# Four graph layers in one launch on one core: the order of norms, biases and kept rows in layer 1, and which banks the sums of layers 3 and 4 use

## The chip, the core and the metric

The kernel runs on 1 core of a Trainium2 chip. The metric is the device time of one launch in microseconds (us). Before the change it is 790.58 us, the median of 3 runs (789.51 to 792.78).

## What is computed

x is 2048 x 256 (f32) and adj is a 2048 x 2048 matrix of zeros and ones. Four layers follow one another, each with a residual and a layer norm:

```python
x = _layernorm(x + _L0_gnn_ref(x, adj, weight, bias, node_w, edge_w))
x = _layernorm(x + _L1_gnn_ref(x, adj, adj, W_sa, a_sa, W_gcnb, b_gcnb, Wa, ba, Wb, bb))
x = _layernorm(x + _L2_gnn_ref(x, adj, weight2))
x = _layernorm(x + _L3_gnn_ref(x, adj, W1, b1, W2, b2, W3, b3))
# layer 1: h = x @ edge_w; e = where(adj > 0, h @ h.T, NEG_BIG)
#   out = (adj * softmax(x @ node_w, axis=0) * softmax(e, axis=1)) @ (x @ weight) + bias
# layer 2: attention over edges plus a plain graph convolution, both gated
# layer 3: relu((D^-1/2 (adj + I) D^-1/2) @ (x @ W))
# layer 4: h = relu(adj @ (x @ W1) + b1); h = relu(adj @ (h @ W2) + b2); adj @ (h @ W3) + b3
```

The code counts layers from 0: `weighted`, `final0` and `round0` are of layer 1, and `aggregate(1, ...)` and `aggregate(2, ...)` of layers 3 and 4.

## The kernel before

Rows of x are cut in 16 tiles of 128 (T = 16) and in 4 blocks of 512 (B = 4, TB = 4 tiles to a block). All order is written out by hand: one instruction stream to each engine, with semaphores between them. PSUM has 8 banks.

**Layer 1** goes tile by tile, t = 0 to 15. TensorE (PE) computes `scores(t)` (line 665), one row tile of h h^T, into banks 0 to 3. The matrix is symmetric, so ScalarE (ACT) keeps the part right of the diagonal in `keep_row(t)` (line 999), and later rows turn it instead of computing it. `make_fill(t)` (line 991) makes the mask from a row tile of adj that GpSimd (POOL) loads in `load_adj` (line 502). VectorE (DVE) adds the mask and takes the maximum in `maxima(t)` (line 1355). ACT takes the exponential (`exp_row`, line 1015) and its f16 high part (`p_high`, line 1020), and DVE the low part (`p_low`, line 1332). SP turns both with DMA transposes (`turn_p`, line 429). `weighted(m)` (line 687) multiplies them with the projected x into bank 6 or 7. `final0(m)` (line 1339) reads that bank, adds x and the bias (`xb`, which POOL makes in `bias_x`, line 497), and takes the moments. POOL makes the reciprocal deviation in `norm_factor` (line 489), and DVE applies it in `normed` (line 1287). PE's turn t is `scores(t)`, then `weighted(SUMMED[t])`, where SUMMED[t] is t - 3 from t = 4 on and 0 for t = 2; `scores(t)` waits for the maximum of t - 1 (`e_read`), and `weighted(m)` for `final0(m - 2)` (`pv_read`). DVE's round t (`round0`, line 1404) is maxima(t), p_low(t - 1), final0 of the tile summed in PE's turn t - 1, then its norm.

Before round 2 stands the start: transposes and projections (`group0`, line 640) through banks 4 to 7, then an exchange of maxima over the partitions on POOL, of which the scale of `sup` is made (lines 1427 to 1435).

**Layers 3 and 4** aggregate block by block. `aggregate(layer, b, f)` (line 783) sums over all 16 tiles, for feature half f = 0 or 1, in bank 4 + f. ACT and DVE take it apart in a high and a low part (`agg_high`, line 1097; `agg_low`, line 1481), and PE goes on with `out2(b)` (line 859) in layer 3 and with `hidden1(b)` and `rows(b)` (lines 880, 891) in layer 4. A sum may start when `agg_lo` says that its bank has been read. Blocks 1 to 3 are a loop on each engine (`Fori`), with this order on PE:

```python
with pe.Fori(1, B) as b:
    aggregate(2, b, 0)
    hidden1(b - 1)
    rows(b - 1, W2s, HID)
    aggregate(2, b, 1)
```

## Time and profile before

| | before |
|---|---|
| median of 3 runs | 790.58 us (789.51 to 792.78) |
| the profiled execution, its own time | 791.85 us |
| its span, first to last instruction | 790.0 us |
| mean granted TensorE clock | 0.988 |
| PE busy | 744.8 us (94%) |
| DVE busy | 452.6 us (57%) |
| ACT busy | 347.4 us (44%) |
| POOL busy | 120.0 us (15%) |

Times in rows count from the start of the span. PE is TensorE's matmuls, DVE VectorE, ACT ScalarE, POOL GpSimd, SPq the DMA queue of SyncE. A bracket at the end of a row of the timeline gives the idle time of the engine before the instruction, and what ended it. Granted clock 1.00 is 2.4 GHz, 0.50 is 1.2 GHz. Layer 1 lasts until 213 us, layer 2 until 391, layer 3 until 463, layer 4 until the end.

### The profile page before, as it was taken

How to read it: one execution, taken by the hardware profiler on the slowest of the kernel's cores; microseconds unless marked ns; L12 is line 12 of the kernel's file. 1: busy time of each engine (PE TensorE's matmuls, PEld its weight loads, DVE VectorE, ACT ScalarE, POOL GpSimd, SP SyncE). 2: the span in 40 equal slices, each digit the busy share in tenths (PEclk: the TensorE clock that was granted, in tenths of full speed). 3: DMA queues.
4: the chain of work that ended last, by engine and by line, in shares of the span. 5: the costliest groups of instructions: out<-in, count | busy, mean ns of one | idle time of the engine just before them, and what ended most of it. 6: DMA issues, size and time to landing. Idle time of an engine off the chain costs nothing.

```text
span 790.0 us, 11567 instructions
## 1 busy us (share of the span) xinstructions
PE 744.8 (94%) x4192; PEld 489.8 (62%) x4192; DVE 452.6 (57%) x934; ACT 347.4 (44%) x530; POOL 120.0 (15%) x246
## 2 busy tenths in 40 slices
PE   7888999797999999999989999999999999999997
PEld 6776766564678878787835545675664546465343
DVE  4485888688768797988944475121271311114465
ACT  4678877675385474646722243132270322224000
POOL 2011222111321012111122340000001000000343
PEclk9998999998999999999999999999999999999999
DMA  8948889996568509400030000000000000000011
GB/s 230 180 91 146 162 164 159 167 155 112 103 95 153 88 2 159 68 2 1 1 87 1 0 0 1 1 0 0 0 0 27 1 1 0 0 0 0 21 41 46
DMA packets 114300, 48.71 MB, mean 62 GB/s; under 512 B 103504, under 2 KB 109776, under 8 KB 114256
## 3 DMA queue, kind: packets, MB, share of 16 engines
q1 hardware_dynamic: 110224, 33.44, 21.7%
q0 software_dynamic: 4032, 14.68, 11.2%
q8 instruction: 27, 0.44, 0.2%
q14 instruction: 17, 0.14, 0.1%
HBM read 35.53 MB, written 2.10 MB: 48 GB/s over the span
## 4 chain that ended last, share of the span: by engine, by line
PE 43%; DVE 7%; issue 3%; ACT 1%; POOL 1%; DVEq 0%; POOLq 0%; ACTq 0%
PE ps L777 11%; PE ps L928 11%; PE ps L904 8%; PE ps L963 4%; PE ps L937 3%; PE ps L887 3%; PE ps L953 2%; DVE stats L1297 1%; PE ps L633 1%; DVE es_lo L1285 1%; DVE x L1575 1%; DVE tm L1495 1%; DVE agg_lo L1483 1%; DVE y L1619 0%; DVE y L1697 0%
## 5 line engine op out<-in xcount | busy, mean ns | idle before, releaser
L777 PE MATMUL ps<-adjT,x 128*128 128x512 bf16 (+1 forms) x768 | 173.3, 379 | 5.1 <-DVE agg_lo L1483 2.5
L777 PEld LDWEIGHTS ps<-adjT,x 128*128 128x128 f16 x768 | 72.3, 98 | 90.4 <-issue 7.6
L696 PE MATMUL ps<-sup,turned 128*128 128x512 f16 x256 | 88.3, 393 | 12.1 <-DVE y L1350 12.1
L1285 DVE TENSOR_TENSOR hh_lo<-hf,hh_hi 128x512 fp32r<-128x512 f32 x32 | 22.2, 693 | 134.5 <-ACT hf L1221 133.5
L928 PE MATMUL ps<-adjT,G 128*128 x384 | 83.6, 379 | 0.4 <-ACT hf L1221 0.4
L819 PE MATMUL ps<-H_hi,es_hi 128*128 128x258 f32 x256 | 76.8, 300 | 2.2 <-DVE es_lo L1285 1.7
L819 PE MATMUL ps<-H_lo,es_hi 128*128 128x258 f32 x256 | 72.4, 283 | 0.0
L819 PE MATMUL ps<-H_hi,es_lo 128*128 128x258 f32 x256 | 72.4, 283 | 0.0
L698 PE MATMUL ps<-sup,turned 128*128 128x256 f16 x256 | 71.7, 280 | 0.0
L928 PEld LDWEIGHTS ps<-adjT,G 128*128 128x128 f16 x384 | 37.3, 98 | 45.4 <-issue 0.9
L492 POOL TENSOR_TENSOR rstd<-mv,epsc 128x1 f32<-128x1 f32 x64 | 15.2, 238 | 295.9 <-DVE mv L1299 295.9
L1106 ACT ACTIVATE es_hi<-tm 128x1024 fp32r<-128x1024 f32 x32 | 33.9, 1059 | 52.6 <-DVE tm L1495 52.4
L696 PEld LDWEIGHTS ps<-sup,turned 128*128 128x128 f16 x256 | 25.7, 100 | 46.9 <-DVE y L1350 14.8
L819 PEld LDWEIGHTS ps<-H_hi,es_hi 128*128 128x128 f32 x256 | 48.3, 189 | 7.7 <-DVE es_lo L1285 4.7
L819 PEld LDWEIGHTS ps<-H_lo,es_hi 128*128 128x128 f32 x256 | 48.5, 189 | 0.4
L819 PEld LDWEIGHTS ps<-H_hi,es_lo 128*128 128x128 f32 x256 | 48.3, 189 | 0.0
L1285 DVE TENSOR_TENSOR es_lo<-tm,es_hi 128x1024 fp32r<-128x1024 f32 x32 | 39.2, 1225 | 14.9 <-issue 6.8
L1483 DVE SCALAR_TENSOR_TENSOR agg_lo<-ps,agg_hi 128x512 fp32r<-128x512 f32 x24 | 16.0, 685 | 52.3 <-ACT agg_hi L1099 52.3
L1328 DVE CUSTOM_DVE_ANT_0 em<-ps,fill 128x1024 f32<-128x1024 f32 x32 | 38.0, 1217 | 13.9 <-ACT kept L1006 7.8
L1495 DVE SCALAR_TENSOR_TENSOR tm<-slrow,ex,nb 128x512 f32<-128x512 f32 x64 | 45.3, 749 | 1.1
L1219 ACT ACTIVATE hh_hi<-ps,b2c,g 128x512 fp32r<-128x512 f32 x16 | 12.5, 779 | 72.2 <-PE ps L928 48.1
L963 PE MATMUL ps<-x,adjT 128*128 128x512 f16 x192 | 41.8, 379 | 1.9 <-DVE y L1699 1.9
(216 smaller groups left out, 1484.7 us busy)
## 6 DMA issues: line engine op xcount, KB each, us to landing
adjb<-in_adj POOLq DMA_DIRECT2D x16, 512.0 KB, 7.0
adjf<-in_adj POOLq DMA_DIRECT2D x12, 512.0 KB, 6.4
x<-in_x SPq DMA_DIRECT2D x4, 512.0 KB, 6.0
out<-adjf SPq DMA_DIRECT2D x16, 128.0 KB, 1.7
adjf<-in_L_gnn_W SPq DMA_DIRECT2D x1, 1024.0 KB, 5.9
W1f<-in_L_gnn_W SPq DMA_DIRECT2D x1, 512.0 KB, 3.7
adjf<-in_L_gnn_W SPq DMA_DIRECT2D x1, 512.0 KB, 3.9
we<-in_L_gnn_edge_w SPq DMA_DIRECT2D x1, 256.0 KB, 3.8
```

Source lines behind the costliest of these rows:

```text
L696: ins = mm(bank(6 + u), PT(HI, t)[:, jt, :], sup[:, jt, :], start=(jt == 0), stop=False, skip_group_check=True)
L698: ins = mm(bank(6 + u, D), PT(LO, t)[:, jt, :], sup[:, jt, 0:D], start=False, stop=(jt == T - 1), skip_group_check=True)
L777: ins = mm(bank(4 + f), x16[:, part, jt, f * P:(f + 1) * P], adj(b, jt), start=(jt == 0 and part == HI), stop=(jt == T - 1 and part == LO))
L819: ins = mm(bank(k, D + 2), es[p][:, (b * T + jt) % RE, k * P:(k + 1) * P], H[q][:, jt, :], start=(jt == 0 and (p, q) == (HI, HI)), stop=(j ...
L904: ins = mm(bank(to, width), hh[p][:, o, k * P:(k + 1) * P], ws[q][:, o, :], start=(o == 0 and (p, q) == (HI, HI)), stop=(o == KH - 1 and p ...
L928: ins = mm(bank(4 + o), g16(jt, part, o * P, P), adj(b, jt), start=(jt == 0 and part == HI), stop=(jt == T - 1 and part == LO))
L963: ins = mm(bank(u), adjT[:, bass.ds(b, 1), jt, k * P:(k + 1) * P].rearrange("p a c -> p (a c)"), f16[:, jt, :], start=(jt == 0), stop=(jt ...
L1106: own.link(run(es[HI][:, s, :], tm[:, s, :], ACT.Exp, scale=SLOPE - 1.0))
L1285: return tt(to, frm, high.bitcast(F32), ALU.subtract)
L1328: nc.vector.tensor_tensor_reduce(out=em[:, u, cols], in0=banks, in1=fill[:, t % 2, cols], scale=1.0, scalar=-3.0e38, op0=ALU.add, op1=ALU.max,
L1483: stt(agg[LO][:, f, :], bank(4 + f), 1.0 / XS, agg[HI][:, f, :].bitcast(F32), ALU.mult, ALU.subtract).then_inc(agg_lo, 1)
L1495: stt(tm[:, (b * T + jt) % RE, :], slrow[:, b * CB:(b + 1) * CB], ex[:, jt, 0:1], nb[:, jt % 2, :], ALU.add, ALU.max).then_inc(tm_ready, 1)
```

## The change

In layer 1:

- x's first block is loaded in two transfers, and the first transposes wait for the first of them (`x_first`) alone.
- `scores(0)` waits block by block for the part of h that it reads, not for all of it.
- On ACT, the mask of tile 1 is made after all projections, row 1 is kept before the exponential of the node weights, row 2 before the exponential of row 1, and row 3 before that of row 2.
- On DVE, the maximum of row 1 stands before the node maximum and the scale. In each round the norm of the former tile stands behind the maximum, and `final0` is of the tile that PE sums in the same turn, at the round's end.
- On POOL the first two biases are added before the exchange, adjacency row 5 is loaded behind it, and row tile 4 for layer 2 is loaded in step 9, not 5. SP turns that tile after all turns of layer 1.

In layers 3 and 4 the sums of odd blocks use banks 6 and 7, those of even blocks 4 and 5; a sum waits for the reading of the block two before. The loops over blocks are written out, the diagonal's waits are per block, and in layer 4 the last of block 2's row tiles stands behind block 3's second sum.

```diff
@@ sums
+        def agg_bank(layer, b, f):
+            return 4 + f + (2 * (b % 2) if layer else 0)
...
-                        wait_from(pe, agg_lo, (layer * B + b) * KD + f - 1)
+                        n = layer * B + b
+                        if n == B + 1:
+                            pe.wait_ge(g_ev, B * TB)
+                        else:
+                            wait_from(pe, agg_lo, (n - 1 if n <= B else n - 2) * KD + f + 1)
...
-            pe.wait_ge(diag_gone, T)
             pe.wait_ge(wp_ready, 2)
-            with pe.Fori(1, B) as b:
+            for b in range(1, B):
+                pe.wait_ge(diag_gone, TB * (b + 1))
                 aggregate(2, b, 0)
                 hidden1(b - 1)
-                rows(b - 1, W2s, HID)
+                rows(b - 1, W2s, HID, tiles=range(TB - (b == B - 1)))
                 aggregate(2, b, 1)
+            rows(B - 2, W2s, HID, tiles=(TB - 1,))
@@ layer 1, VectorE
             def round0(t):
-                u = t % 2
-                maxima(t, u)
-                p_low(t - 1, 1 - u)
-                m = SUMMED.get(t - 1)
-                if m is not None:
-                    final0(m, m % 2)
-                conv_first(LOW_ROUND.get(t, ()))
-                if m is not None:
-                    normed(m, m % 2, x[:, m, :])
+                maxima(t, t % 2)
+                if t - 1 in SUMMED:
+                    m = SUMMED[t - 1]
+                    normed(m, m % 2, x[:, m, :])
+                p_low(t - 1, (t - 1) % 2)
+                conv_first(LOW_ROUND.get(t, ()))
+                if t in SUMMED:
+                    final0(SUMMED[t], SUMMED[t] % 2)
@@ layer 1, the rest
-    LATER_LOADED = {5: 4}
+    LATER_LOADED = {9: 4}
...
+                    if t == 0:
+                        pe.wait_ge(p0_lo, P0.index(("h", c, KD - 1)) + 1)
...
-                if t == T - 2:
-                    sp.wait_ge(e_mm, B * T)
-                    turn_later(TB)
+            sp.wait_ge(e_mm, B * T)
+            for t in (TB, TB + 1):
+                turn_later(t)
```

**DVE, round 8 of layer 1, before** (`em,mx` is the masked maximum, `pl` the low part, `y` and `stats` are of `final0`, `x<-y` is the norm):

```order
L1328 ISA em,mx<-ps,fill 128x1024 [waits s_kept,fill_ready,e_mm]
L1328 ISA mx 128x1
L1328 ISA em,mx<-ps,fill 128x1024 [waits e_mm,s_kept]
L1328 ISA mx 128x1
L1362 TENSOR_SCALAR negm<-mx 128x1 [waits e_read]
L1337 SCALAR_TENSOR_TENSOR pl<-em,ph 128x1024 [waits p_hi,PT_landed1]
...
L1348 SCALAR_TENSOR_TENSOR y<-ps,rowf,xb 128x256 [waits xb_ready,pv_mm,dve_own]
...
L1299 BN_AGGR mv<-stats 128x2 [waits dve_own]
L1290 TENSOR_SCALAR x<-y,mv,rstd 128x256 [waits rstd_ready]
L1328 ISA em,mx<-ps,fill 128x1024 [waits s_kept,fill_ready,e_mm]
```

and the same stretch of the changed kernel:

```order
L1342 ISA em,mx<-ps,fill 128x1024 [waits s_kept,fill_ready,e_mm]
L1342 ISA mx 128x1
L1342 ISA em,mx<-ps,fill 128x1024 [waits e_mm,s_kept]
L1342 ISA mx 128x1
L1376 TENSOR_SCALAR negm<-mx 128x1 [waits e_read]
L1304 TENSOR_SCALAR x<-y,mv,rstd 128x256 [waits rstd_ready]
L1351 SCALAR_TENSOR_TENSOR pl<-em,ph 128x1024 [waits p_hi,PT_landed1]
...
L1362 SCALAR_TENSOR_TENSOR y<-ps,rowf,xb 128x256 [waits xb_ready,pv_mm,dve_own]
...
L1313 BN_AGGR mv<-stats 128x2 [waits dve_own]
L1342 ISA em,mx<-ps,fill 128x1024 [waits s_kept,fill_ready,e_mm]
```

Between the moments (`BN_AGGR`) and the norm that waits for POOL's factor stand now the next round's two maxima.

**ACT, from the scale to round 3, before** (`kept` is `keep_row`, `fill` the mask, `em,Z` the exponential, `ph` the high part):

```order
L1050 ACTIVATE sup<-supf,g 128x4x256 x3
L996 ACTIVATE fill,deg<-adjb 128x2048 [waits e_read,adj_landed2]
L1017 ACTIVATE em,Z<-em,negm 128x2048 [waits e_maxed]
L1006 ACTIVATE kept<-ps 128x512 [waits e_mm] x3
L1028 ACTIVATE ph<-em 128x1024 [waits p_lo,exp_done,PT_landed0]
L1028 ACTIVATE ph<-em 128x1024 [waits p_lo]
L996 ACTIVATE fill,deg<-adjb 128x2048 [waits e_read,adj_landed3]
L1017 ACTIVATE em,Z<-em,negm 128x2048 [waits e_maxed]
```

and now:

```order
L1061 ACTIVATE sup<-supf,g 128x4x256 x3
L1007 ACTIVATE fill,deg<-adjb 128x2048 [waits e_read,adj_landed2]
L1017 ACTIVATE kept<-ps 128x512 [waits e_mm] x3
L1028 ACTIVATE em,Z<-em,negm 128x2048 [waits e_maxed]
L1039 ACTIVATE ph<-em 128x1024 [waits p_lo,exp_done,PT_landed0]
L1039 ACTIVATE ph<-em 128x1024 [waits p_lo]
L1007 ACTIVATE fill,deg<-adjb 128x2048 [waits e_read,adj_landed3]
L1017 ACTIVATE kept<-ps 128x512 [waits e_mm] x3
L1028 ACTIVATE em,Z<-em,negm 128x2048 [waits e_maxed]
```

Rows 2 and 3 are kept ahead of the exponentials of rows 1 and 2.

## Rows read from the trace of the kernel before

**Rows 1.** The page's first part: busy time of each engine.
```profile
PE 744.8 (94%) x4192; PEld 489.8 (62%) x4192; DVE 452.6 (57%) x934; ACT 347.4 (44%) x530; POOL 120.0 (15%) x246
```
**Rows 2.** PE's waits: line, releaser, us in total, times, longest.
```profile
PE ps L696 <- DVE y L1350: 12.1, 8, 4.7
...
PE ps L677 <- DVE mx L1328: 3.1, 1, 3.1
PE ps L633 <- DVE smax L1421: 2.5, 2, 1.7
PE ps L777 <- DVE agg_lo L1483: 2.5, 3, 1.9
...
PE ps L887 <- DVE agg_lo L1483: 1.4, 1, 1.4
PE ps L682 <- DVE hT_lo L1285: 1.4, 1, 1.4
PE ps L777 <- POOL adjT L564: 1.4, 1, 1.4
...
PE ps L682 <- DVE mx L1328: 1.1, 1, 1.1
```
**Rows 3.** Windows: length, busy PE, PEld, DVE, ACT, POOL, granted clock, DMA share, GB/s.
```profile
72.00:78.00 6.00, 6.00 (x17) 4.89 (x18) 4.75 (x10) 3.50 (x5) 1.67 (x2) 0.52 0.73 159
78.00:121.70 43.70, 43.70 (x259) 30.34 (x258) 36.71 (x78) 33.82 (x42) 8.20 (x16) 1.00 0.90 163
...
156.00:160.00 4.00, 3.85 (x13) 1.84 (x14) 2.87 (x7) 2.14 (x3) 1.99 (x4) 0.57 1.12 212
...
192.00:193.50 1.50, 1.40 (x5) 0.72 (x6) 1.32 (x6) 0.74 (x2) 0.52 (x2) 0.50 1.12 214
193.50:200.00 6.50, 6.50 (x33) 3.39 (x31) 5.04 (x10) 0.42 (x1) 1.22 (x2) 0.71 1.21 186
```
**Rows 4.** DVE's timeline, one round: start, us, instruction, idle before and releaser.
```profile
127.94 1.21 DVE L1328 CUSTOM_DVE_ANT_0 em<-ps,fill 128x1024 f32<-128x1024 f32 x1
...
136.11 0.81 DVE L1290 TENSOR_SCALAR x<-y,mv,rstd 128x256 f32<-128x256 f32 x1 [0.95 <-POOL rstd L493]
136.85 1.21 DVE L1328 CUSTOM_DVE_ANT_0 em<-ps,fill 128x1024 f32<-128x1024 f32 x1
```
**Rows 5.** PE's timeline: first instruction of turns 11 and 12; two waits.
```profile
139.64 1.26 PE L677 MATMUL ps<-ident,kept 128*128 128x128 f32 x10
...
148.55 1.47 PE L677 MATMUL ps<-ident,kept 128*128 128x128 f32 x12
...
192.10 0.61 PE L696 MATMUL ps<-sup,turned 128*128 128x512 f16 x1 [3.87 <-DVE y L1350]
```
**Rows 6.** POOL's, SP's and DVE's timelines around the longest of these waits.
```profile
137.32 0.54 POOL L535 DMA_DIRECT2D adjf<-in_adj  x1
...
141.76 5.46 SPq L433 DMA_TRANSPOSE turned<-pl  x1
...
152.18 1.23 DVE L1337 SCALAR_TENSOR_TENSOR pl<-em,ph 128x1024 f16<-128x1024 f32 x1 [3.81 <-DMA turned<-pl]
```
**Rows 7.** DVE's, ACT's and PE's timelines around rounds 3 to 5.
```profile
70.61 1.23 DVE L1328 CUSTOM_DVE_ANT_0 em<-ps,fill 128x1024 f32<-128x1024 f32 x1 [4.88 <-ACT kept L1006]
...
77.79 2.01 ACT L1028 ACTIVATE ph<-em 128x1024 f16<-128x1024 f32 x2 [2.42 <-DMA turned<-ph]
79.70 0.47 ACT L1006 ACTIVATE kept<-ps 128x384 f32<-128x384 f32 x1
...
84.50 0.71 PE L677 MATMUL ps<-ident,kept 128*128 128x128 f32 x5
```
**Rows 8.** DVE's and PE's timelines in layers 3 and 4.
```profile
459.39 0.69 DVE L1483 SCALAR_TENSOR_TENSOR agg_lo<-ps,agg_hi 128x512 fp32r<-128x512 f32 x1 [0.53 <-ACT agg_hi L1099]
...
460.18 0.35 PE L633 MATMUL ps<-wls_hi,agg_hi 128*128 128x256 f32 x1 [1.46 <-issue]
...
479.40 0.39 PE L777 MATMUL ps<-adjT,x 128*128 x1 [1.92 <-DVE agg_lo L1483]
```

More of the change, by code:

```diff
@@ L335, in build @@
         f16 = x16[:, :, :, :].rearrange("p a t d -> p (a t d)").rearrange("p (t c) -> p t c", t=T)
-        x_landed = [sem(f"x_landed{c}") for c in range(B)]
+        x_first, x_landed = sem("x_first"), [sem(f"x_landed{c}") for c in range(B)]
         we_landed, we_ready = sem("we_landed"), sem("we_ready")
@@ L399, in _ @@
             x_tiles = x_in.rearrange("(t p) d -> p t d", p=P)
+            sp.dma_start(x[:, 0:2, :], x_tiles[:, 0:2, :]).then_inc(x_first, 16)
             for c in range(B):
-                sp.dma_start(x[:, TB * c:TB * c + TB, :], x_tiles[:, TB * c:TB * c + TB, :]).then_inc(x_landed[c], 16)
+                tiles = slice(TB * c if c else 2, TB * c + TB)
+                sp.dma_start(x[:, tiles, :], x_tiles[:, tiles, :]).then_inc(x_landed[c], 16)
                 if c == 0:
@@ L439, in _ @@
                 turn_p(t, LO)
-                if t == T - 2:
-                    sp.wait_ge(e_mm, B * T)
-                    turn_later(TB)
-            for t in (TB + 1,):
+            sp.wait_ge(e_mm, B * T)
+            for t in (TB, TB + 1):
                 turn_later(t)
@@ L512, in _ @@
             pool.wait_ge(w0_landed, 48)
-            for t in range(AB + 2):
+            for t in range(AB + 1):
                 load_adj(t)
+            bias_x(0, 0)
+            bias_x(1, 1)
             pool.wait_ge(node_max, 1)
@@ L520, in _ @@
             nc.gpsimd.partition_all_reduce(nst[:, 4:5], nst[:, 3:4], P, RADD).then_inc(node_sum, 1)
-            for t in range(AB + 2, 2 * AB):
+            for t in range(AB + 1, 2 * AB):
                 load_adj(t)
-            bias_x(0, 0)
-            bias_x(1, 1)
             def load_later(t):
@@ L776, in aggregate_tiles @@
                     for part in (HI, LO):
-                        ins = mm(bank(4 + f), x16[:, part, jt, f * P:(f + 1) * P],
+                        ins = mm(bank(agg_bank(layer, b, f)), x16[:, part, jt, f * P:(f + 1) * P],
                                  adj(b, jt), start=(jt == 0 and part == HI),
@@ L889, in hidden1, with rows @@
                     ins.then_inc(h_mm, 1)
-            def rows(b, ws, width, last=False, uncounted=0):
-                for k in range(TB):
+            def rows(b, ws, width, last=False, uncounted=0, tiles=range(TB)):
+                for k in tiles:
                     n = b * TB + k
@@ L911, in _ @@
                     aggregate_tiles(2, 0, f, (jt,))
-            pe.wait_ge(diag_gone, T)
             pe.wait_ge(wp_ready, 2)
-            with pe.Fori(1, B) as b:
+            for b in range(1, B):
+                pe.wait_ge(diag_gone, TB * (b + 1))
                 aggregate(2, b, 0)
                 hidden1(b - 1)
-                rows(b - 1, W2s, HID)
+                rows(b - 1, W2s, HID, tiles=range(TB - (b == B - 1)))
                 aggregate(2, b, 1)
+            rows(B - 2, W2s, HID, tiles=(TB - 1,))
             hidden1(B - 1)
@@ L1067, in _ @@
                     make_fill(t + 1)
+                if t + 1 == TB - 1:
+                    keep_row(t + 1)
                 exp_row(t)
@@ L1098, in agg_high @@
                 act.wait_ge(agg_mm, (layer * B + b) * KD + f + 1)
-                run(agg[HI][:, f, :], bank(4 + f), ACT.Copy, scale=1.0 / XS).then_inc(agg_hi, 1)
+                run(agg[HI][:, f, :], bank(agg_bank(layer, b, f)), ACT.Copy, scale=1.0 / XS).then_inc(agg_hi, 1)
             def edge_exp(b, pair):
@@ L1193, in _ @@
             agg_high(1, 0, 0)
-            with act.Fori(1, B) as b:
+            for b in range(1, B):
                 agg_high(1, b - 1, 1)
@@ L1221, in hidden, with rows @@
                 run(hf[:, o % 2, :], bank(frm), ACT.Relu, bias=bias[:, o:o + 1], scale=scale).then_inc(h_f, 1)
-            def rows(b, to, first, width):
-                for k in range(TB):
+            def rows(b, to, first, width, tiles=range(TB)):
+                for k in tiles:
                     act.wait_ge(r_mm, b * TB + k + 1)
@@ L1230, in mid @@
                     hidden(b, o, o % 2, b1c, 1.0)
-                rows(b, G, AHEAD, HID)
+                rows(b, G, AHEAD, HID, range(TB - (b == B - 2)))
             agg_high(2, 0, 0)
-            with act.Fori(1, B) as b:
+            for b in range(1, B):
                 agg_high(2, b - 1, 1)
@@ L1238, in _ @@
             agg_high(2, B - 1, 1)
+            rows(B - 2, G, AHEAD, HID, (TB - 1,))
             for o in range(KH):
@@ L1445, in _ @@
                     weight_parts()
+            conv_first(range(9, 12))
             p_low(T - 1, 1)
-            conv_first(range(9, 11))
-            final0(T - 4, 0)
-            conv_first(range(11, 12))
             normed(T - 4, 0, x[:, T - 4, :])
@@ L1482, in agg_low @@
                 dve.wait_ge(agg_hi, (layer * B + b) * KD + f + 1)
-                stt(agg[LO][:, f, :], bank(4 + f), 1.0 / XS, agg[HI][:, f, :].bitcast(F32),
+                stt(agg[LO][:, f, :], bank(agg_bank(layer, b, f)), 1.0 / XS, agg[HI][:, f, :].bitcast(F32),
                     ALU.mult, ALU.subtract).then_inc(agg_lo, 1)
@@ L1626, in _ @@
             agg_low(1, 0, 0)
-            with dve.Fori(1, B) as b:
-                own.enter(b - 1, TB)
+            for b in range(1, B):
                 agg_low(1, b - 1, 1)
@@ L1631, in _ @@
                 agg_low(1, b, 0)
-            own.leave(B - 1)
             agg_low(1, B - 1, 1)
@@ L1667, in _ @@
             weight_bound(0, W2f)
-            with dve.Fori(1, B) as b:
+            for b in range(1, B):
                 agg_low(2, b - 1, 1)
```

22 lines of the change are left out of this document (11 added, 11 removed).

## The prediction

> **What bounds the kernel now.** I read the page's busy times first, then PE's waits, then windows for the granted clock, and the timelines of layer 1 last. PE is busy 94% of the span, DVE 57% [rows 1], so the kernel is bound by PE's own work, and a change of order can only win back what PE loses in waits and in clock. The list of PE's waits shows where that is [rows 2]. In layer 1 there are 12.1 us in eight waits of `weighted` for `final0` (L1350), 3.1 and 1.1 us for a maximum (L1328), 2.5 us for the projections' banks (L1421) and 1.4 us for h: 20.2 us in all. In layers 3 and 4 there are 2.5 us for `agg_lo` before a sum (L777), 1.4 us for the diagonal and 1.4 us for `agg_lo` before `hidden1` (L887): 5.3 us.
>
> The windows add the clock [rows 3]. After the 3.1 us wait, PE ran at 0.52 of its clock for 6 us, which costs 6 x 0.48 = 2.9 us. After the 4.7 us wait it ran at 0.57 for 4 us (1.7 us). After the 3.9 us wait at 192.1 [rows 5] it ran at 0.50 for 1.5 us and at 0.71 for 6.5 us (0.75 + 1.9 us). That is 7.2 us more, lost at the level of 1.2 GHz, each time behind a wait of 3 us or longer. What layer 1 can give is so 20.2 + 7.2 = 27.4 us.
>
> Who is late in layer 1? DVE's round is 136.85 - 127.94 = 8.91 us, and it contains one idle stretch, the 0.95 us in which the norm waits for POOL's factor [rows 4]. PE's turn takes the same 8.91 us (148.55 - 139.64) [rows 5] and contains one of the eight waits. Without the longest two these are 12.1 - 4.7 - 3.9 = 3.5 us in six, 0.6 us each. So from round 8 on DVE is the bound, by a little: PE's own work in a turn is about 8.3 us, DVE's is 8.91 - 0.95 = 7.96 us. Between 78 and 121.7 us it is PE alone that bounds, busy 43.7 of 43.7 us, with the DMA engines at 0.90 [rows 3].
>
> **The change in layer 1, until round 5.** `scores(0)` no longer waits for all of h. The last block is needed only by its fourth bank, and it is ready 1.4 us after PE's arrival, while three banks are being computed: -1.4 us. The mask of tile 1 leaves the middle of the projections, where it stood behind the high part in the longer of the two waits of 2.5 us in all. The other wait is behind the exponential and stays. High part and exponential still cut in, so I give this 0.9 of the 2.5 us (bounds 0 and 1.7, the longer wait). The maximum of row 1 moves ahead of the scale: the wait of 1.1 us for it becomes one for the kept row 1, which now ends last, and I take 0.3 us. What this delays is the scale itself, hence `sup`; `weighted(0)` needs its four pieces one after another, and PE has `scores(2)` before it as cover. Without that cover it would cost those 0.3 us again. The kept row 3 moves ahead of an exponential. In its place DVE was idle 4.9 us, waiting for that row [rows 7]. Now DVE is late instead, because `final0(0)` stands ahead of the maximum of row 3. The 3.1 us wait becomes 2.9: -0.2 us. The clock's 2.9 us I count as won, since the next item shows that a loss there costs nothing.
>
> This brings PE to turn 5 at 84.5 - 1.4 - 0.9 - 0.3 - 0.2 - 2.9 = 78.8 us instead of 84.5 [rows 7]. But the maximum of row 4 is behind the high part that waits at 77.79 for the landing of the former one [rows 7], a chain of DMA transposes that this change hardly moves. From 79.7 the first piece of the kept row takes 0.47 us, then the first half of the maximum 1.2: 81.4 us. So 2.6 us are given back, and 5.7 - 2.6 = **3.1 us** are won by turn 5. The split of x's first load, the two biases on POOL and adjacency row 5 behind the exchange I cost at nothing. The two biases run while POOL waits for ACT and DMA; row 5 is needed two rounds later. For the split, between a second transfer's delay and a start of PE 1 us earlier, I bound it by +0.5 and -0.5 us.
>
> **From round 5 on.** The norm behind the next maximum takes the 0.95 us idle out of DVE's round: 7.96 us against PE's 8.3. PE bounds, and the six short waits go (3.5 us). `weighted(m)` also gets `final0(m - 2)` a round earlier in program order, so the longest wait cannot come from DVE's backlog. The 4.7 us wait has a cause of its own [rows 6]. At 137.32 POOL issued row tile 4 of layer 2 (`adjf`, 512 KB), right behind an adjacency row of the same size. The transposes behind them took 5.46 us to issue, and DVE waited 3.81 us for the landing. Row tile 4 now goes in step 9, where no adjacency row is loaded, so this wait goes as well (4.7 + 1.7 us of clock). The 3.9 us wait at 192 us is DVE's backlog of conversions ahead of `final0`, gone with it 0.75 + 1.9 us of clock. Together 3.5 + 6.4 + 6.5 = 16.4 us. Not all of it: in the last turns PE turns most of its scores from kept rows and is quicker than 8.3 us, DVE has the conversions on top, and the last two low parts must land before `weighted(14)` and `weighted(15)`. That price no row shows. Its ends are 0 and 7.7 us (3.8 + 3.9, were both landings as late as the one in [rows 6]); I take 2.4 us, by the wait for a landing that follows directly on another transpose [rows 7]. So **14.0 us**. SP's turn of tile 4 moves from between two turns of layer 1 to behind them: POOL, which waits for it before it loads tile 5, is then held for up to 3 us, and `norm_factor(14)` is queued behind it. Both tiles belong to block 1 of layer 2, and PE and DVE have all of block 0 before it, so I cost it at nothing.
>
> A word on one duration. The norm takes 0.81 us [rows 4], beside POOL's addition of the bias. The Trainium skill (SBUF — State Buffer, "The single rule") has VectorE and GpSimd share a port pair, with the second to come fully blocked, if VectorE's instruction is in a two-port mode; the maximum, with one input in PSUM, would not contend. By it the norm in its new place takes about half as long, and DVE's round is some 0.4 us shorter still. The sum does not change by this, since PE bounds.
>
> **Layers 3 and 4.** With two pairs of banks a block's first sum waits for the reading of the block two before. The 2.5 us of waits (1.92 of them at 479.4 [rows 8]) go; at each the other pair was long free. The 1.4 us for the diagonal go, since block 1's part was added long before. Before `hidden1(3)` stands now a row tile's products, 12 matmuls of 512 columns; at the 43.7 / 259 = 0.17 us of the dense stretch [rows 3], where many are narrower, that is 2 us, more than the 1.4 us that it covers. Not touched is the 1.46 us at 460.18, named "issue": DVE's `agg_lo` ends there at 459.39 + 0.69 [rows 8], and `out2(3)` needs it as before. Won: 2.5 + 1.4 + 1.4 = **5.3 us**. The other engines' loops written out cost nothing that a row shows; layer 1 is written out and PE runs it without a gap [rows 3].
>
> **Sum.** 3.1 + 14.0 + 5.3 = 22.4 us. Against the profiled execution (791.85 us) that is 769.4; it stood 1.27 us above the median, so against the median 790.58 it is **768.2 us**. A measurement of this kernel can tell about 0.5% (4 us) from no change.
>
> **Rivals.**
> - The DMA queue binds (0.15). DMA work in a round with a load is 0.90 of (121.7 - 84.5) / 4 = 9.3 us [rows 3, 7], 8.4 us; PE's turn is 8.3 us and less. For: a share of 1.12 and late landings whenever two loads meet [rows 3, 6]. Against: from step 8 on only one load is left. Then the 4.7 us wait and its 1.7 us of clock come back in another place: 768.2 + 6.4 = 774.6 us.
> - VectorE stays the bound (0.12). `final0` now waits for the sum of the same turn, and the next maximum stands behind it. For: DVE's 7.96 us are 0.3 us from PE's. Against: after a sum's end PE has scores and a sum before it needs that maximum. Then the six short waits stay: 771.7 us.
> - The second pair of banks gives nothing (0.06): the 5.3 us turn up at the next reader of `agg_lo`, as at 460.18 [rows 8]. 773.5 us. The Trainium skill (TensorE: Matmul & The Clock Gate, "HAM oscillation — how this bites in real kernels") reports a kernel in which double buffering in PSUM gave no further gain. The trace speaks against it here, since these waits have the buffer itself as their end.
> - The given-back 2.6 and 2.4 us don't come (0.06): 763.2 us.
> - Slower (0.03): the written-out loops starve PE of instructions. Second and third passes are 2 x (64 + 24) + 2 x (64 + 24 + 48) = 448 matmuls that now are fetched anew. From 50 ns lost at each the gain is gone, at 60 ns it is 790.6 - 22.4 + 26.9 = 795.1 us. Against: the dense, written-out stretch of layer 1 [rows 3]. The Trainium skill (Runtime: NRT & Kernel Launch, "Instruction fetch mechanics") says that fetch is sequential and mostly hidden, and that branches are what stalls it.
>
> **Numbers.** The forecast has 0.58. Range: below, 763.2 less the split's 0.5 and the 1.7 us of the first bound reaches 761; above, the DMA rival with a little of the second reaches 777. Outside are the slower case and mixtures. Faster by over 0.5%: all but the slower rival and 0.02 of mixtures, 0.95; within 0.5%: 0.02; slower: 0.03.
>
> **What would show it.** Right: no wait of `weighted` over 1 us between rounds 6 and 13, PE's turns 8.3 to 8.6 us there, granted clock 1.00 from 85 to 180 us, layer 1 over by 196 us, and no L777 wait for `agg_lo` or the diagonal in layers 3 and 4. A wait for a kept row or a maximum at turn 5 should be new. Wrong: transposes that land late in each round, DVE without idle time, or gaps named "issue" in the written-out blocks.

## The result, and the profile after

The changed kernel takes 780.23 us, the median of 4 runs (777.92 to 783.60), beside 791.68 us of the kernel before (789.51 to 792.83, 4 runs on the same chip). The ratio is 0.9851, with a 95% interval of 0.9814 to 0.9887: faster by 11.5 us. Forecast were 768.2 us and 22.4 us. In this document a ratio and its interval leave out executions more than 1.5% slower than the fastest of the same kernel, while medians and the ranges in brackets are of all executions.

| | after |
|---|---|
| the profiled execution, its own time | 778.83 us |
| its span | 777.0 us (before 790.0) |
| mean granted TensorE clock | 0.995 (before 0.988) |

PE's waits of the changed kernel (line, releaser, us in total, times, longest) answer to [rows 2]:

```profile
PE ps L683 <- DVE mx L1342: 7.7, 6, 3.1
PE ps L702 <- DMA turned<-pl: 5.4, 4, 2.8
...
PE ps L683 <- ACT kept L1017: 2.7, 3, 1.2
...
PE ps L638 <- DVE smax L1435: 1.3, 2, 0.8
```

The 12.1 us for `final0` are gone, and so are the three lines on `agg_lo` and the diagonal. In their place stand three others that were not there or were shorter: maxima (4.2 us before, now 7.7), kept rows, and landings (the end of a DMA transfer) of the low part's transposes.

The windows of layer 1 and of the last stage (columns as in [rows 3]):

```profile
62.00:85.00 23.00, 16.21 (x85) 11.77 (x85) 13.12 (x23) 18.66 (x22) 2.69 (x5) 1.00 0.83 148
85.00:165.00 80.00, 76.15 (x465) 52.16 (x464) 67.89 (x146) 58.59 (x72) 16.66 (x34) 1.00 0.97 158
165.00:205.00 40.00, 34.78 (x242) 22.82 (x241) 35.03 (x84) 21.34 (x33) 11.01 (x19) 1.00 0.79 145
...
735.00:777.00 42.00, 36.35 (x160) 15.90 (x160) 23.27 (x59) 0.00 (x0) 15.79 (x35) 0.92 0.12 42
```

No stretch of layer 1 at 1.2 GHz is left. But PE stands still for 3.85 of the 80 us in the middle, where I expected nothing.

PE's timeline there, and at the end of the layer: the first instruction of turns 5, 6, 10 and 12, then that of `weighted(14)`, with the idle time before it.

```profile
82.28 0.74 PE L683 MATMUL ps<-ident,kept 128*128 128x128 f32 x5 [3.12 <-DVE mx L1342]
...
93.20 0.85 PE L683 MATMUL ps<-ident,kept 128*128 128x128 f32 x6 [1.14 <-DVE mx L1342]
...
130.55 1.09 PE L683 MATMUL ps<-ident,kept 128*128 128x128 f32 x8 [0.92 <-ACT kept L1017]
...
149.30 1.09 PE L683 MATMUL ps<-ident,kept 128*128 128x128 f32 x8 [1.17 <-ACT kept L1017]
...
191.50 0.38 PE L702 MATMUL ps<-sup,turned 128*128 128x512 f16 x1 [2.82 <-DMA turned<-pl]
```

With the same marks of the kernel before this gives where the gain lies (us, from both timelines):

| stretch | before | after | gain | forecast |
|---|---|---|---|---|
| until turn 5 starts | 84.50 | 82.28 | 2.2 | 3.1 |
| turns 5 to 13 | 86.23 | 83.20 | 3.0 | |
| turn 14 to the end of layer 1 | 42.41 | 38.94 | 3.5 | |
| (both) | | | 6.5 | 14.0 |
| layers 2 to 4, until the last stage | 536.5 | 530.5 | 6.0 | 5.3 |
| last stage | 40.4 | 42.0 | -1.7 | 0 |

The sum is 13.0 us, the difference of the spans of these two executions. The largest part of the miss is turns 5 to 13: 7.3 us were to be won there and 3.0 were. At the end of the layer it is 6.7 and 3.5 us, in the last stage 0 and -1.7. Such marks are those of single executions: layer 1 of the kernel before ended at 213.1 us here and at 221.4 us in another execution of the same code (`sums_alone`, below).

Here is the middle of layer 1. First SP and POOL: start, length of the issue.

```profile
114.79 1.98 SPq L439 DMA_TRANSPOSE turned<-pl  x1
...
118.14 0.59 POOL L512 DMA_DIRECT2D adjb<-in_adj  x1
...
118.80 5.47 SPq L439 DMA_TRANSPOSE turned<-ph  x1
...
124.42 3.08 SPq L439 DMA_TRANSPOSE turned<-pl  x1
```

Then ACT, and the second half of DVE's maximum of row 9:

```profile
116.77 2.00 ACT L1039 ACTIVATE ph<-em 128x1024 f16<-128x1024 f32 x2 [2.91 <-DMA turned<-ph]
...
127.74 2.00 ACT L1039 ACTIVATE ph<-em 128x1024 f16<-128x1024 f32 x2 [3.80 <-DMA turned<-ph]
...
129.65 0.85 ACT L1017 ACTIVATE kept<-ps 128x256 f32<-128x256 f32 x2
...
130.67 1.22 DVE L1342 CUSTOM_DVE_ANT_0 em<-ps,fill 128x1024 f32<-128x1024 f32 x1 [2.60 <-issue]
```

This is a chain that the prediction did not have in the middle of the layer. `final0` now stands at the round's end. POOL's factor, bias and load follow it, and so adjacency row 12 is issued 0.66 us ahead of the high part's transposes (before, the loads stood 0.88 to 1.94 us behind them in seven of eight rounds, and every such set landed 6.2 to 6.7 us after its issue). Here they need 5.47 us to issue and land 8.9 us after they started. ACT's next high part waits 3.80 us for that, and the kept row is queued behind it. The second half of the maximum starts 0.17 us after the end of that kept row, with DVE idle for 2.60 us, and `scores(10)` starts 0.92 us late.

Turn 12 is of the same kind, but there the load stood 0.68 us behind the transposes of 137.97 us. These landed after 8.8 us, ACT waited 4.29 us and PE 1.17. The 1.14 us at turn 6 are another matter: DVE waited 0.75 us for a landing at 84.28 us and from then until that maximum had no idle time, since the products of layer 2's weights (`weight_products`, 2.9 us) stand ahead of it. That wait is VectorE's own work.

### The profile page after: what moved, and what is told of

The parts are those of the page before. It is cut to its first block, busy times and chain, and to the rows that moved or that the text cites. A ratio compares the mean times of both kernels' runs of the same rounds, so it can differ in the third digit from the quotient of the medians.

```text
span 777.0 us, 11259 instructions
## 1 busy us (share of the span) xinstructions
PE 739.4 (95%) x4192; PEld 486.3 (63%) x4192; DVE 447.6 (58%) x934; ACT 346.1 (45%) x530; POOL 121.9 (16%) x246
## 3 DMA queue, kind: packets, MB, share of 16 engines
q0 software_dynamic: 4032, 14.68, 11.5%
## 4 chain that ended last, share of the span: by engine, by line
PE 45%; DVE 6%; issue 2%; ACT 1%; POOL 0%; POOLq 0%; ACTq 0%; DVEq 0%
PE ps L787 11%; PE ps L939 11%; PE ps L914 9%; PE ps L974 5%; PE ps L948 3%; PE ps L897 3%; PE ps L964 2%; PE ps L638 1%; DVE stats L1311 1%; DVE es_lo L1299 1%; DVE tm L1507 1%; DVE x L1587 1%; ACT x L1142 0%; PE ps L829 0%; DVE y L1709 0%
## 5 line engine op out<-in xcount | busy, mean ns | idle before, releaser
L787 PE MATMUL ps<-adjT,x 128*128 128x512 bf16 x768 | 172.8, 380 | 1.5 <-DVE x L1587 1.2
L702 PE MATMUL ps<-sup,turned 128*128 128x512 f16 x256 | 84.2, 380 | 5.4 <-DMA turned<-pl 5.4
L704 PE MATMUL ps<-sup,turned 128*128 128x256 f16 x256 | 69.8, 273 | 0.0
L1299 DVE TENSOR_TENSOR es_lo<-tm,es_hi 128x1024 fp32r<-128x1024 f32 x32 | 39.2, 1225 | 14.8 <-issue 6.8
L974 PE MATMUL ps<-x,adjT 128*128 128x512 f16 x192 | 43.5, 390 | 1.9 <-DVE y L1709 1.9
```

Source lines behind the costliest of these rows:

```text
L702: ins = mm(bank(6 + u), PT(HI, t)[:, jt, :], sup[:, jt, :], start=(jt == 0), stop=False, skip_group_check=True)
L704: ins = mm(bank(6 + u, D), PT(LO, t)[:, jt, :], sup[:, jt, 0:D], start=False, stop=(jt == T - 1), skip_group_check=True)
L787: ins = mm(bank(agg_bank(layer, b, f)), x16[:, part, jt, f * P:(f + 1) * P], adj(b, jt), start=(jt == 0 and part == HI), stop=(jt == T - 1 ...
L974: ins = mm(bank(u), adjT[:, bass.ds(b, 1), jt, k * P:(k + 1) * P].rearrange("p a c -> p (a c)"), f16[:, jt, :], start=(jt == 0), stop=(jt ...
L1299: return tt(to, frm, high.bitcast(F32), ALU.subtract)
```

## The experiments

Two theories at first. **Q**: the place of the load beside the high part's transposes makes these late, and ScalarE's order carries that to PE. **V**: VectorE's own work still bounds. Later two readings of the DMA engines' side: **C**, their total work in a round is too much; **D**, the distance between the two issues decides. All ratios are to the kernel before, timed beside them. Marks and waits are of the one profiled execution of each kernel.

### The parts of the change

`sums_alone`: the kernel before with the edits of layers 3 and 4.

```diff
+            return 4 + f + (2 * (b % 2) if layer else 0)
...
-            with pe.Fori(1, B) as b:
+            for b in range(1, B):
```

> The kernel before with the change of layers 3 and 4 alone (two pairs of banks, loops written out, last row tile of block 2 behind the second sum). The gains of the two halves of the change add up, as the two profiles suggest: 5.9 us, so 785.8 us, layer 1 over at 213 us as before. Rival: the written-out loops or the second banks have a cost that layer 1's gain hides: 788 us or more.

Measured: 787.52 us (785.27 to 798.32), ratio 0.9939 (0.9917 to 0.9961): 4.8 us, where 5.9 were expected. Layer 1 was not over at 213 us in the profiled execution (794.24 us) but at 221.4, with the same layer 1 as before. A load 0.29 us behind a set of transposes explains a large part of it:

```profile
116.23 1.88 SPq L437 DMA_TRANSPOSE turned<-ph  x1
...
116.52 0.59 POOL L512 DMA_DIRECT2D adjb<-in_adj  x1
...
132.80 2.00 ACT L1037 ACTIVATE ph<-em 128x1024 f16<-128x1024 f32 x2 [9.13 <-DMA turned<-ph]
```

These transposes landed after 16.6 us, and PE waited 4.83 us for the kept row behind that high part and then ran at 0.77 of its clock from 135 to 150 us. No set met such a load in the profile of the kernel before. `layer1_alone` is the other half, the changed kernel with layers 3 and 4 as before.

> The changed kernel with layers 3 and 4 as before. Layer 1 over at 204.4 us, as in the changed kernel; by the two marks (213.1 and 204.4) it is worth 8.7 us: 783.0 us. If the last stage takes part of it back, as in the profile of the changed kernel (1.7 us): 784.7 us.

Measured: 785.90 us (782.79 to 787.89), 0.9918 (0.9894 to 0.9941): 6.5 us. The halves add up to 11.3 us, the whole change has 11.8 by its ratio. Nothing in layers 3 and 4 is paid for by layer 1. Its layer 1 ended at 204.5 us, as expected, but 783.0 us were expected too: the profiled execution (782.79 us) is the fastest of the six and 3.1 us below their median, so its marks promise more than the median keeps.

### VectorE's order and the second load

`round_before`: the changed kernel with VectorE's rounds in the old order. (Here and in the kernels with the kept row ahead, VectorE also waits for its own low part of two rows before, long done by then.)

```diff
                maxima(t, u)
-                if t - 1 in SUMMED:
-                    normed(m, m % 2, x[:, m, :])
-                p_low(t - 1, (t - 1) % 2)
-                conv_first(LOW_ROUND.get(t, ()))
-                if t in SUMMED:
-                    final0(SUMMED[t], SUMMED[t] % 2)
+                p_low(t - 1, 1 - u)
+                if m is not None:
+                    final0(m, m % 2)
+                conv_first(LOW_ROUND.get(t, ()))
+                if m is not None:
+                    normed(m, m % 2, x[:, m, :])
```

> The changed kernel with VectorE's round in the order of before (maximum, low part, the sum's reading, its norm). Theory Q (order in the DMA queue): in the changed round POOL issues the adjacency row just ahead of the transposes of the high part, in the old one just behind them. So here those transposes issue in 2.0 us again and ScalarE's high part does not wait for a landing; turns 5 to 14 take 80 us instead of 83.2, but the wait of 3.9 us at the layer's end comes back with its clock: layer 1 over at 204 to 205 us, time within 1 us of the changed kernel. Theory V (VectorE's own work bounds): turns 5 to 14 take 83 us or more and the layer's end is later by 3.5 us: 782 to 784 us.

(The same order is restored behind the last round.) Measured: 781.34 us (780.24 to 784.20), 0.9861 (0.9838 to 0.9884), within 1.1 us of the changed kernel. The time is what Q gave, the marks are not: in the profiled execution, the slowest of the six, turns 5 to 13 take 85.4 us instead of 80 and layer 1 ends at 211.6 us instead of 204 to 205, with waits for `final0` of 4.4 us in all between 85 and 165 us. Two loads were issued 0.39 and 0.12 us behind the high part's transposes there. So with the second load moved away, the new order, the main part of the change in layer 1, brings nothing more that these times can tell: it trades waits for `final0` against waits for kept rows.

`load_step5` moves row tile 4 of layer 2 back behind an adjacency row.

```diff
-    LATER_LOADED = {9: 4}
+    LATER_LOADED = {5: 4}
```

> The changed kernel with row tile 4 of layer 2 loaded in step 5 again, right behind an adjacency row. It should bring back a long landing (5.5 us of issue, 4 to 5 us of PE's wait, and clock behind it): 5 to 6 us slower than the changed kernel, 785.5 us. Rival: in the changed order two loads in a row are one collision as any other and cost nothing more: 780 us.

Measured: 781.23 us (778.92 to 781.48), 0.9832 (0.9789 to 0.9875). The rival holds. The two loads do collide (the transposes behind them take 7.09 us to issue, ACT waits 4.56 us), but PE waits 1.94 us where it waited 4.7. The 4.7 us went with the old order too, in which `final0` stood behind the low part that waited 3.81 us for the landing [rows 6]. So the new order and the later load each do the work of the other. The old order with the early load and the rest of the change was not run.

### The load itself

`no_loads` leaves out the loads of adjacency rows 8 to 15: the mask is made of an earlier row's data.

```diff
-                if t + 2 * AB < T:
-                    load_adj(t + 2 * AB)
```

> The changed kernel without the loads of adjacency rows 8 to 15 (row r is masked with row r - 4's or an earlier one's data, so the output is not the reference's). Bounds what the loads' collisions cost. Theory D and C alike: the high part's transposes issue in 2 us, no wait of ScalarE for a landing, PE's turns equal its own work (79.4 us from turn 5 to 14), 4 us less than the changed kernel, a little more if the waits at the layer's end are due to loads too. Theory V (VectorE bounds): no gain.

Measured: 771.80 us (771.00 to 772.69), 0.9725 (0.9683 to 0.9766). That is 1.3% below the changed kernel's ratio, and the intervals do not touch: 8 to 10 us, twice the 4 expected. Between 85 and 165 us PE has no wait at all; turns 5 to 13 take 79.8 us, 3.4 less. The end of the layer is 3.5 us shorter too (35.5 us), with landings of 1.39 and 1.03 us before `weighted(14)` and `weighted(15)`, and the last stage takes 40.4 us instead of 42.0, of which below. The windows of turns 6 to 13 of the changed kernel and of this one:

```profile
93.20:165.50 72.30, 69.58 (x428) 48.24 (x429) 60.64 (x128) 53.29 (x63) 14.87 (x31) 1.00 0.97 157
```
```profile
94.27:163.00 68.73, 68.73 (x430) 48.38 (x429) 63.19 (x134) 56.82 (x66) 12.18 (x25) 1.00 0.72 126
```

PE's own work is 68.73 / 8 = 8.6 us a turn, from 9.4 at turn 6 to 7.7 at turn 13. VectorE's work fits in it, so V falls for these turns as a whole. (Turn 6 is no test of it: behind a wait of 3.83 us at turn 5 PE came 1.1 us later to it than in the changed kernel.) The mean busy share of the DMA engines comes to 0.72 x 8.6 = 6.2 us a turn without the load and 0.97 x 9.04 = 8.8 us with it. That 8.8 is more than 8.6 was my reason for C; `kept_first` below decides it.

`load_behind_ph` was meant to cure it: the load waits until the high part is written.

```diff
+                    pool.wait_ge(p_hi, 2 * (t + 3) + 2)
                     load_adj(t + 2 * AB)
```

> The changed kernel, and POOL issues adjacency row t + 8 only when the high part of the same round is written, so that its transposes stand first in the DMA queue. Theory Q: they issue in 2.0 us instead of 4.4 to 5.6, no wait of the high part for a landing over 1 us between 85 and 160 us, turns 5 to 14 take 79.5 to 80.5 us instead of 83.2, time 3 us less than the changed kernel. Theory C (the DMA engines' total work per round binds, the order does not matter): the low part's transposes are late instead, turns 5 to 14 stay at 83 us, no gain. Theory V (VectorE bounds): no gain.

Measured: 837.97 us (834.19 to 838.91), 1.0571 (1.0546 to 1.0595): 57 us slower than the changed kernel, all of it in layer 1, which ended at 261.3 us. No theory had that. The transposes of the high part do issue in 2.0 us. But in each round the load is issued 0.27 us behind them, and then (issues of 93 to 213 us: count, KB, median us to landing) all three transfers take about twice as long as in the next kernel:

```profile
adjb<-in_adj POOLq DMA_DIRECT2D x7, 512.0 KB, 14.2
turned<-ph SPq DMA_TRANSPOSE x7, 15.0
turned<-pl SPq DMA_TRANSPOSE x7, 11.9
```

`load_1us_behind` has the same wait and puts the addition of the bias between it and the load, 0.7 us.

```diff
+                    pool.wait_ge(p_hi, 2 * (t + 3) + 2)
                 if t + 2 < T:
                     bias_x(t + 2, t % 2)
                 if t + 2 * AB < T:
                     load_adj(t + 2 * AB)
```

> As the kernel with the load behind the high part, but with the addition of the bias between that wait and the load, so that the load is issued some 1.0 us behind the high part's transposes instead of 0.27, as it was in the kernel before (1.04 and 1.14). Theory D: the landings of 14 to 16 us go, and with them all or most of the 58 us; at or a little below the changed kernel. Rival: it is the waiting itself, which lets ScalarE, SP and POOL hold one another once per round, whatever the distance: 820 us or more.

Measured: 779.93 us (776.80 to 781.90), 0.9826 (0.9779 to 0.9874). All 58 us are back, for a distance of 0.72 to 0.81 us in seven rounds instead of 0.27:

```profile
adjb<-in_adj POOLq DMA_DIRECT2D x6, 512.0 KB, 7.9
turned<-pl SPq DMA_TRANSPOSE x8, 5.7
turned<-ph SPq DMA_TRANSPOSE x7, 7.0
```

The two kernels wait for the same semaphore, so the waiting itself, the rival, is out, and D holds for this extreme. `load_at_mask` puts the load ahead of `norm_factor`.

```diff
+                if 0 < t < T - 2 * AB:
+                    load_adj(t + 2 * AB)
                 norm_factor(t, t % 2)
```

> The changed kernel, and POOL loads adjacency row m + 8 ahead of norm_factor(m) instead of behind norm_factor(m) and bias_x: as soon as the mask that frees its slot is made, 2.5 to 3 us behind the high part's transposes and as much ahead of the low part's. Theory D (what counts is the distance between the load's issue and that of a set of transposes; 0.3 us behind them both took 14 to 16 us to land): no landing later than 7 us, ScalarE's high part never waits over 1 us for one between 100 and 160 us, turns 5 to 14 take 80 us, time 3 us less than the changed kernel. Theory C (total DMA work of a round binds): turns 5 to 14 stay at 83 us, and the low part's transposes land late instead.

Measured: 778.69 us (774.53 to 784.61), 0.9806 (0.9762 to 0.9851), not to be told from the changed kernel. The profiled execution (784.61 us) is the slowest of the six. The landings were not all under 7 us: loads 2.9 to 3.4 us behind the transposes left them at 4.3 us, but row 11's was issued 0.22 us behind a set of them. These landed after 11.2 us, ACT waited 8.70 and PE 3.83 us. Another, 0.67 us behind, cost 9.4 us of landing and 1.47 us of PE.

### The way to PE

`norm0_behind` concerns turn 5.

```diff
                 maxima(t, t % 2)
+                if t == 3:
+                    p_low(t - 1, (t - 1) % 2)
                 if t - 1 in SUMMED:
...
-                p_low(t - 1, (t - 1) % 2)
+                if t != 3:
+                    p_low(t - 1, (t - 1) % 2)
```

Its reason is in the timelines of DVE, POOL and ACT of the changed kernel:

```profile
65.01 0.53 POOL L512 DMA_DIRECT2D adjb<-in_adj  x1 [6.87 <-ACT fill L1007]
...
75.18 0.18 POOL L496 TENSOR_TENSOR rstd<-mv,epsc 128x1 f32<-128x1 f32 x1 [9.64 <-issue]
...
76.01 0.73 POOL L504 TENSOR_TENSOR xb<-x,brow 128x256 f32<-128x256 f32 x1
...
76.06 0.82 DVE L1304 TENSOR_SCALAR x<-y,mv,rstd 128x256 f32<-128x256 f32 x1 [6.89 <-POOL rstd L497]
...
78.13 2.11 ACT L1039 ACTIVATE ph<-em 128x1024 f16<-128x1024 f32 x2 [4.17 <-DVE pl L1351]
```

> The changed kernel, but in round 3 alone the norm of tile 0 stands behind the low part of row 2, as in the kernel before. In the changed kernel that norm waits 6.9 us for POOL's factor (POOL stands still for 9.6 us after its last exchange), and the low part of row 2, the high part of row 3, the kept row 4 and its maximum stand behind it in a chain. Theory N: the wait of 3.1 us at turn 5 goes, PE reaches turn 5 at 79 us instead of 82.3, and layer 1 ends 3 us sooner: 777 us. Rival (the landing of the transposes of row 2 is late anyway, as I forecast): turn 5 at 81.4 us or later, gain 1 us or none.

Measured: 785.53 us, 0.9867 (0.9815 to 0.9920), from 778.38 to 794.62; the ratio is of four executions (778.38 to 789.13), and they show no gain. The rival is right. In the profiled execution (790.47 us) ACT's high part of row 3 waits 3.26 us for the landing of row 2's transposes, and PE still waits 1.93 us at turn 5, which starts at 82.28 us as before this edit. It also shows an accident: row 13's load came 0.33 us behind a set of transposes at 128.79, these landed after 14.5 us, and PE waited 7.2 us.

`kept_first` takes the kept row out of the high part's queue.

```diff
                 exp_row(t)
+                if TB - 1 <= t < T - 1:
+                    keep_row(t + 1)
                 p_high(t)
```

> The changed kernel, but ScalarE keeps row t + 1 ahead of the high part of row t (from round 3 on), so a high part that waits for a landing no longer holds the kept row, the maximum and PE's scores. Theory Q (the landing reaches PE only by way of the kept row): no wait of PE for a kept row or a maximum from turn 5 to 14, these turns take 79.5 to 80.5 us instead of 83.2; the high part is later, so its transposes move away from the load, which is issued first. With 2 of the 3.1 us at turn 5: 774 to 776 us. Rival: the delay comes back by VectorE, whose low part waits for the later high part and holds the next maximum: 780 us or more.

Measured: 778.22 us (775.16 to 780.53), 0.9816 (0.9778 to 0.9853), as a time not to be told from the changed kernel. ACT's high part still waits for landings (3.34 us once), but from turn 7 to turn 13 PE has no wait and these turns take 59.4 us, as without the loads (59.3), instead of 62.8. The windows of these seven turns, changed kernel and this one:

```profile
102.64:165.48 62.84, 60.13 (x373) 41.38 (x372) 51.67 (x109) 45.65 (x54) 12.86 (x27) 1.00 0.99 161
```
```profile
105.53:164.91 59.38, 59.38 (x372) 41.48 (x371) 50.74 (x108) 45.01 (x54) 12.96 (x27) 1.00 1.05 174
```

Q holds in these turns: it is the kept row by which the landing reaches PE. And C falls: all loads are there, the DMA engines' share is 1.05, which is 8.9 us a turn, and PE is busy for 59.38 of 59.38 us. (A share above 1 stands in [rows 3] as well, so a share times a turn is no amount that has to fit in the turn.) The 3.4 us are in part given up at turn 6, where PE waits 2.8 us and then runs at 1.2 GHz for a while, since VectorE's low part of row 3 waits for a landing ahead of the maximum. That is the rival, in one place.

`kept_norm0` has both edits.

> Both edits: the kept row ahead of the high part, and the norm of tile 0 behind the low part of row 2. If they act in different places (turn 5, and turns 6 to 14), they add up: layer 1 over at 197 to 198 us, 772 to 774 us. If both only free the kept row 4, no better than the better of the two alone.

Measured: 775.54 us (771.52 to 790.94), 0.9757 (0.9717 to 0.9798), beside 772 to 774 expected. This is below the changed kernel with intervals apart (0.9757 against 0.9851, about 7 us), 19 us below the kernel before. In the profiled execution no wait is left at turn 5, and turns 5 to 11 take 63.1 us instead of 67.0. Then one load was issued 0.01 us ahead of a set of transposes, and a wait of another kind came, followed by one at the end of the layer, both for the low part:

```profile
149.30 0.38 PE L702 MATMUL ps<-sup,turned 128*128 128x512 f16 x1 [2.50 <-DMA turned<-pl]
...
189.66 0.58 PE L702 MATMUL ps<-sup,turned 128*128 128x512 f16 x1 [3.69 <-DMA turned<-pl]
```

So in this execution layer 1 ended at 204.3 us, not at the 197 to 198 I expected, although the gain at turn 5 and that of turns 6 to 11 did add up.

`tail_low` adds, in round 15, the low part of row 14 ahead of the maximum.

```diff
+                if t == T - 1:
+                    p_low(t - 1, (t - 1) % 2)
                 maxima(t, t % 2)
```

> The kernel with the kept row ahead and the norm of tile 0 behind, and in round 15 the low part of row 14 ahead of the maximum of row 15. At the end of layer 1 PE waited 3.7 us for the landing of this low part's transposes before weighted(14); it was written at 185.1 us, 2.6 us behind where VectorE could have it. Expected: that wait 1.3 us, layer 1 over 2 us sooner, 773.5 us. Rival: the maximum of row 15, its exponential and high part are 2.3 us later, and weighted(15) waits for them instead: no gain.

Measured: 774.44 us (770.48 to 785.41), 0.9783 (0.9762 to 0.9804): not to be told from the kernel without the edit. In the profiled execution layer 1 ended at 201.6 us. The landing no longer ends that wait, but `final0(12)`, queued behind more work, does (2.67 us). So in this execution VectorE stands right behind the transfer at the end of the layer.

`tail_load` issues the load ahead of the bias in that kernel.

```diff
+                if t + 2 * AB < T:
+                    load_adj(t + 2 * AB)
                 if t + 2 < T:
                     bias_x(t + 2, t % 2)
```

> As that kernel, and POOL issues the adjacency row between the norm's factor and the addition of the bias, 0.7 us sooner. Theory D (a load that starts within some 0.3 us behind a set of transposes takes 14 to 16 us to land with them, one 0.7 to 1 us behind 7 to 9 us, one 2 us ahead 6 us): the loads then stand 2.4 to 3 us ahead of the high part's transposes and no longer meet them, no landing over 8 us, PE without a wait from turn 5 to 14, and the runs lie closer together: 771 to 773 us. Theory C (the total of the round's DMA work): no different from the kernel without this edit.

Measured: 777.07 us (776.04 to 780.28), 0.9833 (0.9813 to 0.9852). No gain, rather 4 us lost. The runs do lie closer together, but landings of 8 us are as frequent (8.8 us with the load 2.1 us ahead), and PE waits 4.07 and 2.48 us. Neither wait speaks for C. From turn 7 to 13 PE has none, with a DMA share of 1.06 and turns that take 59.3 us. The 4.07 us at turn 6 stand behind VectorE's low part of row 3, which waited 3.11 us for a landing, and the load there was issued 0.66 us behind that set of the low part's transposes. The 2.48 us at 175.09 follow row tile 4's load, issued 0.36 us behind a set, which landed after 11.3 us. So taking the load from one set of transposes moved it towards another, and the edit does not show a free place for it in every round.

## Why the prediction was wrong

**Turn 5.** The sum until PE's arrival was 5.7 us, and it measured 5.3 (79.16 instead of 84.50); h with x's split load gave 1.8 us, the projections 1.3. That 2.6 us would be given back at a maximum was right in place and too small: 3.1 us. It named the landing as the cause. Two causes lie there on top of each other. The norm of tile 0, moved ahead of the low part, waits 6.9 us for POOL, which the prediction did not look at. With it gone, the landing of which I spoke still holds PE 1.93 us.

**The middle.** This is the step that failed: "DVE's round: 7.96 us against PE's 8.3. PE bounds, and the six short waits go". PE did not bound. What could be won there was 0.9 (three short waits) + 4.7 + 1.7 = 7.3 us. It was won but for 0.45 us of the clock, and 3.86 us of other waits came in: 1.14 at turn 6 behind VectorE's own work, 0.92 + 0.31 at turn 10 and 1.17 + 0.31 at turn 12 behind a late landing, by way of ACT's high part, the kept row and the maximum. `no_loads` takes all of these away, and `kept_first` those of turns 10 and 12 with the loads in place.

I had come near with the first rival, "the DMA queue binds", at 0.15 and 6.4 us. Its working does not stand: 8.4 us were set against a turn of 8.3, but they are of turns 5 to 8 of the kernel before, of which PE's own work filled 9.3 us each (43.7 of 43.7 us busy [rows 3]), and at 8.9 us a turn in `kept_first` the DMA engines bound nothing. Late landings in single rounds were the cause, not the queue's total. Against the rival I held that from step 8 on only one load is left. The waits came before it, at turns 6 to 12, with one adjacency row loaded beside each turn, and one load is enough. In the sum I never followed that load through the change. It hangs on `final0` by way of POOL, so moving `final0` moved it: in the round of row 12 from 1 us behind the high part's transposes to just ahead of them, in the others to between 2.0 us ahead and 1.9 us behind. I looked at queues only for the instructions that the diff moves, not for those that follow them.

Of the signs that I named, no wait of `weighted` over 1 us in rounds 6 to 13 and a granted clock of 1.00 came true. Turns of 8.3 to 8.6 us (7.7 to 9.8) and the layer's end at 196 us (204.4) did not. The first could not: without any wait, in `no_loads`, the same turns take 9.4 to 7.7 us. The 8.3 us were worked out from one turn and taken for all.

**The 6.4 us of the two loads** were won, but not only for the reason given: put together again, the loads cost the changed kernel 1 us, within the intervals. With the new order of VectorE's round they no longer reach PE as they did.

**The end of layer 1.** This is a term of the wrong size. 2.6 us (three short waits) + 3.9 + 2.65 us were to go and 2.4 us to be given back, 6.7 us won. The waits for landings there are 0.46 + 2.82 + 1.03 us, 4.3 in all, with 0.9 us for a kept row and a maximum at turn 15 (0.59 + 0.31), and 0.45 us less of clock came back. So the stretch gained 3.5 us.

**Layers 3 and 4.** 5.3 us forecast, 6.0 by the marks, 4.8 alone by the ratio. From the end of layer 1 to the last stage it is 536.1 and 536.5 us in the two traces without this half of the change, and 530.4 to 530.9 us in the other thirteen. The untouched wait stands, as said:

```profile
448.74 0.36 PE L638 MATMUL ps<-wls_hi,agg_hi 128*128 128x256 f32 x1 [1.46 <-issue]
```

The rival that written-out loops starve PE and the one that the second banks give nothing are both out.

**The last stage** took 1.7 us more at a granted clock of 0.92, with the same instructions. It is not the change: in all 15 traces this stage takes either 40.3 to 40.4 us (eleven) or 42.0 to 42.1 us (four), and `kept_first` and others with the same code there are among the short ones. What decides between the two stays open.

**The norm** takes 0.40 us in its new place, not 0.81:

```profile
121.73 0.40 DVE L1304 TENSOR_SCALAR x<-y,mv,rstd 128x256 f32<-128x256 f32 x1
```

The one of tile 0, which ran beside POOL's addition (the rows on turn 5 above), took 0.82, and one more beside it, at 198.42 us, 0.80. By the rule of the Trainium skill (SBUF — State Buffer, "The single rule") that VectorE and GpSimd share a port pair, this is as expected, and the trace agrees.

## What to carry to other kernels

When an instruction moves, follow not only what it releases but what stands in the same queues behind those, DMA issues above all: here a load moved by 1.7 us in one round without a line of its own in the diff. Do not take a high share of the DMA engines for a bound: at 0.99 PE lost 2.7 us in seven turns, at 1.05 nothing. Ask instead which landing an engine waits for, and what stands queued behind it. Keep what the critical engine needs (the kept row) ahead of whatever waits for a landing.

## What was not expected of the hardware

**Two transfers issued together.** These are the 146 sets of the high part's transposes in the 15 traces between 75 and 172 us, with their issue to landing beside the distance of the nearest load's issue:

| load's issue against that of the transposes | sets | landing after, us: least, median, most |
|---|---|---|
| none from 4 us ahead to 2.9 us behind | 37 | 4.3, 4.3, 10.4 (next after a set of 14.5) |
| 1.2 to 4 us ahead | 38 | 4.5, 6.6, 8.8 |
| 0.9 us ahead to 0.12 us behind | 16 | 7.2, 8.8, 9.3 |
| 0.22 to 0.39 us behind | 10 | 10.0, 14.8, 16.6 |
| 0.48 to 0.78 us behind | 15 | 6.0, 7.9, 9.4 |
| 0.8 to 2.6 us behind | 30 | 4.3, 6.7, 8.4 |

A distance of 0.2 to 0.4 us is far worse than both less and more. Five of these ten sets are of `load_behind_ph`, the others of five other kernels. The Trainium skill (DMA: Bandwidth & Descriptors, "Issuing engines are not separate DMA queues") says that transfers of different engines interleave on the same 16 DMA engines. That fits the other rows, in which both share the time; it does not give the 15 us. Why they arise is open. It may be why runs of one kernel differ by 15 us (`norm0_behind`): a small shift decides whether a round meets this distance. One pair of traces bears this out: with the same layer 1, the kernel before met it nowhere and ended the layer at 213.1 us, and `sums_alone` met it once (0.29 us) and ended it at 221.4. That all such differences come from it is not shown.

**POOL's standstill.** In 14 of the 15 traces POOL does nothing for 9.6 to 10.4 us after its third exchange and the loads behind it, with nothing to wait for, until its first elementwise instruction (75.18 above; before, 9.84 us at 76.19). The Trainium skill (GPSIMD Engine Reference, "2.1 Instruction dispatch") tells of about 6 us, without an instruction in the profile, at the first call to freshly loaded code. No run here varied it, so that cause was not tested.
